# Carrying the gate in every feature: one 512-column pass a tile in the aggregation of a graph layer

## The reference

```python
xn  = layernorm(x)
neigh = xn[dst]
w   = sigmoid(relu(neigh @ W1 + b1) @ W2 + b2)     # one gate a node
num = segment_sum(neigh * w, src)                  # 256 sums a node
den = segment_sum(w, src)                          # one sum a node
out = where(den > 0, num / max(den, 1e-12), 0)
x2  = x + out + mix(xn)
```

## Time and profile before

| | |
|---|---|
| median of 3 runs | 1849.69 us |
| the profiled execution, its own time | 1852.44 us |
| its span, first to last instruction | 1850.3 us |
| TensorE busy (matmul) | 1487.4 us, 80% |
| VectorE busy | 1346.5 us, 73% |
| ScalarE busy | 820.7 us, 44% |
| matmuls of `aggregate` | 4802 |
| mean granted TensorE clock | 0.915 of full speed |

### The profile page before, as it was taken

One profiled execution on the slowest core, in us unless ns is written; L12 is line 12 of the kernel. 1 busy time (PEld: TensorE's weight loads), 2 busy tenths in 40 slices (PEclk: granted clock), 3 DMA queues, 4 the chain that ended last, 5 costly groups with the idle time before them and its releaser, 6 DMA issues.

```text
span 1850.3 us, 40316 instructions
## 1 busy us (share of the span) xinstructions
PE 1487.4 (80%) x12157; PEld 1373.1 (74%) x12157; DVE 1346.5 (73%) x3891; ACT 820.7 (44%) x1979; POOL 750.7 (41%) x727
## 2 busy tenths in 40 slices
PE   0327776755659999999999999999999659999897
PEld 0226665644549988888888989888888649998786
DVE  6966999989937777777777777776777546676555
ACT  1114343424635555454544454544545325554443
POOL 1497677774431222222212122222213143337776
PEclk9958787856779999999999999999999869999999
DMA  7000000002334110110101010110101055543442
GB/s 173 12 0 1 1 1 1 1 3 78 129 100 142 37 43 35 37 43 31 46 31 48 31 43 34 43 37 32 45 31 48 35 168 138 138 117 96 121 124 77
DMA packets 68021, 108.67 MB, mean 59 GB/s; under 512 B 14164, under 2 KB 47707, under 8 KB 67705
## 3 DMA queue, kind: packets, MB, share of 16 engines
q1 hardware_dynamic: 49720, 56.19, 11.1%
q0 software_dynamic: 18240, 51.74, 7.9%
HBM read 52.41 MB, written 57.47 MB: 59 GB/s over the span
## 4 chain that ended last, share of the span: by engine, by line
PE 59%; issue 15%; POOL 9%; DVE 8%; ACT 3%; DMA 3%; SPq 1%; DVEq 1%; another core or an unknown queue 0%; POOLq 0%; ACTq 0%
PE turned L1386 17%; PE front L1386 15%; PE turned L1368 9%; POOL acc_mem L766 5%; DVE sort_mem L1674 4%; PE turned L1522 4%; PE front L1522 4%; PE front L1542 4%; ACT a_ring L1124 2%; POOL tab_mem L752 2%; DMA gath_mem<-in_dst 1%; PE front L1415 1%; PE turned L1515 1%; PE front L1420 1%; DVE sort_mem L1682 1%
## 5 line engine op out<-in xcount | busy, mean ns | idle before, releaser
L1780 DVE TENSOR_TENSOR sort_mem<-lane_bf,sort_mem 128x512 bf16<-128x512 bf16 x1372 | 500.3, 406 | 204.8 <-PE turned L1368 190.2
L1124 ACT ACTIVATE a_ring<-turned 128x512 fp32r<-128x512 f32 (+2 forms) x686 | 368.8, 544 | 442.1 <-PE turned L1368 437.4
L1386 PE MATMUL turned<-y_all,a_ring 128*128 128x258 f32 x2450 | 388.9, 296 | 30.6 <-ACT a_ring L1124 30.6
L1386 PE MATMUL front<-y_all,a_ring 128*128 128x258 f32 x2352 | 378.9, 298 | 13.0 <-ACT a_ring L1124 11.8
L1386 PEld LDWEIGHTS turned<-y_all,a_ring 128*128 128x128 f32 x2450 | 317.6, 190 | 36.4 <-ACT a_ring L1124 33.7
L1674 DVE TENSOR_TENSOR sort_mem<-sort_mem 128x320 f32<-128x320 f32 (+2 forms) x568 | 326.8, 637 | 3.0
L1386 PEld LDWEIGHTS front<-y_all,a_ring 128*128 128x128 f32 x2352 | 305.9, 189 | 27.7 <-ACT a_ring L1124 23.7
L1368 PE MATMUL turned<-sort_mem 128*128 128x128 bf16 (+1 forms) x2695 | 258.9, 217 | 2.7 <-DVE sort_mem L1780 2.5
L851 POOL COPY feat_mem<-node_id 128x1 int32 (+1 forms) x49 | 9.0, 183 | 445.7 <-DVE list_at L1889 445.7
L1368 PEld LDWEIGHTS turned<-sort_mem 128*128 128x128 bf16 x2695 | 147.8, 98 | 36.6 <-DVE sort_mem L1780 3.6
L2070 DVE COPY acc_mem<-feat_mem 128x1796 f32 x112 | 122.7, 1098 | 24.8 <-issue 24.8
(11 more groups left out here) (256 smaller groups left out, 2293.5 us busy)
## 6 DMA issues: line engine op xcount, KB each, us to landing
base<-token_lists SPq DMA_DIRECT2D x54, 258.0 KB
base<-token_lists SPq DMA_DIRECT2D x54, 130.0 KB
gated_rows<-tab_mem SPq DMA_DIRECT2D x49, 128.5 KB, 2.9
late_mem<-mixed_rows SPq DMA_DIRECT2D x49, 128.0 KB
mixed_rows<-base SPq DMA_DIRECT2D x12, 512.0 KB, 3.5
feat_mem<-in_L_ffn_expert_w SPq DMA_DIRECT2D x18, 256.0 KB, 6.1
base<-in_x SPq DMA_DIRECT2D x1, 3136.0 KB
base<-in_x SPq DMA_DIRECT2D x1, 2352.0 KB
```

Of the source, the lines that this page charges most:

```text
L1124: nc.scalar.activation(a_ring[:, k % 2, :, :].rearrange("p s n -> p (s n)")[:, 0:width], ps_a[k % 2][:, 0:width], ACT.Copy).then_inc(S["a_ ...
L1386: last = nc.tensor.matmul(ps_agg[odd], a_ring[:, k % 2, n, :], y_part(t, part), start=(t == 0 and part == 0), stop=(t == BLOCKS - 1 and pa ...
L1780: nc.vector.tensor_tensor(hot[:, k % 2, 0:pairs, 0:lanes, :], lane_bf[:, 0:lanes, :].unsqueeze(1).broadcast_to([P, pairs, lanes, 2]), edge ...
```

## The change

Both parts become 256 columns wide, so that a tile of `y_all` is 512 columns, and one matmul of 512 columns takes the place of two of 258. Its output fills one PSUM bank: the sums of the high parts on the left, of the low parts on the right. The gate's column leaves `y_all`. Instead the gate is added to every feature (`y_bias` becomes `(x_bias + 1) * gate`), so a row is `gate * (xn + 1)`. As the features of xn sum to zero, the sum over all 512 columns is 256 times the sum of the gates: ScalarE takes it while it copies the sums, with `accum_out`. VectorE makes minus a 256th of it and the larger of a 256th and 1e-12 (two small operations at step 4), the reciprocal at step 5, joins high part, low part and the negative at step 6, and makes x2 at step 7. Y_TILE goes from 516 to 512.

```diff
-PART = DIM + 2
-Y_TILE = 2 * PART
+Y_TILE = 2 * DIM
...
-LEAD = dict(den=4, over_den=5, x2=6, stats=8, ...
+LEAD = dict(den=4, over_den=5, join=6, x2=7, stats=8, ...
...
-        sums = dense(ROW)
+        sums = dense(Y_TILE)
...
-        ps_agg = [turned[:, 2 * BANK:2 * BANK + PART], bank(3)[:, 0:PART]]
+        ps_agg = [turned[:, 2 * BANK:2 * BANK + Y_TILE], bank(3)[:, 0:Y_TILE]]
...
-        N_NORM, N_ROUTE = 4, 9
-        X2_LINK = 3
+        N_NORM, N_ROUTE = 6, 9
+        JOIN_LINK, X2_LINK = 4, 5
...
             nc.gpsimd.tensor_tensor(y_scale, x_rstd, gate, ALU.mult).then_inc(S["y_params"], 1)
-            nc.gpsimd.tensor_tensor(y_bias, x_bias, gate, ALU.mult).then_inc(S["y_params"], 1)
+            nc.gpsimd.tensor_scalar(y_bias, x_bias, 1.0, None, ALU.add).then_inc(S["y_params"], 1)
+            pool.wait_ge(S["y_params"], 2)
+            nc.gpsimd.tensor_tensor(y_bias, y_bias, gate, ALU.mult).then_inc(S["y_params"], 1)
...
-                nc.gpsimd.tensor_tensor(y_part(t, 1), y_out[:, t % Y_SLOTS, :], y_part(t, 0).bitcast(F32), ALU.subtract)...
+                nc.gpsimd.tensor_tensor(y_part(t, 1), y_out[:, t % Y_SLOTS, 0:DIM], y_part(t, 0).bitcast(F32), ALU.subtract)...
...
-                nc.scalar.activation(y_part(t, 0), y_out[:, s, :], ACT.Copy).then_inc(S["hi_ready"], 1)
+                nc.scalar.activation(y_part(t, 0), y_out[:, s, 0:DIM], ACT.Copy).then_inc(S["hi_ready"], 1)
...
-                    act.wait_ge(S["norm_step"], N_NORM * (rounds - 2) + X2_LINK)
-                nc.scalar.activation(sums, ps_agg[1 - odd][:, 0:ROW], ACT.Copy).then_inc(S["sums_kept"], 1)
+                    act.wait_ge(S["norm_step"], N_NORM * (rounds - 2) + JOIN_LINK)
+                nc.scalar.activation(sums, ps_agg[1 - odd], ACT.Copy, accum_out=den[:, 0:1]).then_inc(S["sums_kept"], 1)
...
-                    for part in range(2):
-                        last = nc.tensor.matmul(ps_agg[odd], a_ring[:, k % 2, n, :], y_part(t, part), start=(t == 0 and part == 0),
-                                                stop=(t == BLOCKS - 1 and part == 1))
+                    last = nc.tensor.matmul(ps_agg[odd], a_ring[:, k % 2, n, :], y_parts(t), start=(t == 0), stop=(t == BLOCKS - 1))
...
-                        nc.vector.tensor_scalar(den[:, 0:1], sums[:, DIM:ROW], 1e-12, None, ALU.max).then_inc(S["norm_step"], 1)
+                        weight, share = den[:, 0:1], 1.0 / DIM
+                    nc.vector.tensor_scalar(den[:, 1:2], weight, -share, None, ALU.mult).then_inc(S["norm_step"], 1)
+                    nc.vector.tensor_scalar(den[:, 2:3], weight, share, 1e-12, ALU.mult, ALU.max).then_inc(S["norm_step"], 1)
+                if j == LEAD["over_den"]:
+                    dve.wait_ge(S["norm_step"], links + 2)
...
+                    nc.vector.reciprocal(den[:, 3:4], den[:, 2:3]).then_inc(S["norm_step"], 1)
+                if j == LEAD["join"]:
...
+                        nc.vector.scalar_tensor_tensor(x2[slot], sums[:, 0:DIM], den[:, 1:2], sums[:, DIM:Y_TILE], ALU.add,
+                                                       ALU.add).then_inc(S["norm_step"], 1)
                 if j == LEAD["x2"]:
+                    dve.wait_ge(S["norm_step"], links + JOIN_LINK)
...
-                    nc.vector.scalar_tensor_tensor(x2[slot], of, den[:, 1:2], mixed_in[slot], ALU.mult, ALU.add)...
+                    nc.vector.scalar_tensor_tensor(x2[slot], x2[slot], den[:, 3:4], mixed_in[slot], ALU.mult, ALU.add)...
```

More of the change, by code:

```diff
@@ L134 @@
 RUNS = ((0, 4), (4, 8), (8, 12), (12, GROUP))
-LEAD = dict(den=4, over_den=5, x2=6, stats=8, spread=10, norm=17, turn=18, turned=19, router=21, hidden=22, logits=24,
+LEAD = dict(den=4, over_den=5, join=6, x2=7, stats=8, spread=10, norm=17, turn=18, turned=19, router=21, hidden=22, logits=24,
             peak=28, exp=30, probs=37, top=40, top_exp=42, index=43, share=46, marks=48, rank=50, place=54)
@@ L215 @@
 assert HALF // 2 < TAIL < HALF // 2 + 2 * P
-SCRATCH = 25 * Y_TILE + PART
+SCRATCH = 13158
 GATHERED = GROUP * ROW
@@ L273, in y_part, with y_parts @@
         def y_part(t, k):
-            at = home_of_tile(t) * Y_TILE + k * PART
-            return y_all[:, at:at + PART]
+            at = home_of_tile(t) * Y_TILE + k * DIM
+            return y_all[:, at:at + DIM]
+        def y_parts(t):
+            at = home_of_tile(t) * Y_TILE
+            return y_all[:, at:at + Y_TILE]
         mixed_in = [late_mem[:, s * DIM:(s + 1) * DIM] for s in range(2)]
@@ L426, in gps_layer @@
         to_lane, round_up, round_down = (in_front(1) for _ in range(3))
-        den, stats, mean_var, rstd, logit_max, exp_l = (after(n) for n in (2, 6, 2, 2, 1, EXPERTS))
+        den, stats, mean_var, rstd, logit_max, exp_l = (after(n) for n in (4, 6, 2, 2, 1, EXPERTS))
         exp_sum, top, top_i, top_f, top_w = after(2), after(8), after(8).bitcast(U32), after(2), after(3)
@@ L1818, in normalise @@
                         dve.nop().then_inc(S["slot_free"], 1)
-                        nc.vector.tensor_scalar(den[:, 0:1], acc_mem[:, bass.ds(ROW * b + DIM, 1)], 1e-12, None, ALU.max).then_inc(S["norm_step"], 1)
+                        weight, share = acc_mem[:, bass.ds(ROW * b + DIM, 1)], 1.0
                     else:
                         dve.wait_ge(S["sums_kept"], n + 1)
-                        nc.vector.tensor_scalar(den[:, 0:1], sums[:, DIM:ROW], 1e-12, None, ALU.max).then_inc(S["norm_step"], 1)
-                    dve.wait_ge(S["norm_step"], links + 1)
-                    dve.nop().then_inc(S["slot_free"], 1)
-                if j == LEAD["over_den"]:
-                    nc.vector.reciprocal(den[:, 1:2], den[:, 0:1]).then_inc(S["norm_step"], 1)
+                        weight, share = den[:, 0:1], 1.0 / DIM
[3 more added lines that the diff above has]
+                    dve.wait_ge(S["norm_step"], links + 2)
+                    dve.nop().then_inc(S["slot_free"], 1)
+                    nc.vector.reciprocal(den[:, 3:4], den[:, 2:3]).then_inc(S["norm_step"], 1)
+                if j == LEAD["join"]:
+                    if not isinstance(listed, int) or listed > 0:
+                        dve.wait_ge(S["row_listed"], 32 * listed)
+                        dve.nop().then_inc(S["slot_free"], 1)
+                    if cut_path:
+                        nc.vector.tensor_scalar(x2[slot], acc_mem[:, bass.ds(ROW * b, DIM)], den[:, 1:2], None, ALU.add).then_inc(S["norm_step"], 1)
+                    else:
+                        nc.vector.scalar_tensor_tensor(x2[slot], sums[:, 0:DIM], den[:, 1:2], sums[:, DIM:Y_TILE], ALU.add,
+                                                       ALU.add).then_inc(S["norm_step"], 1)
                 if j == LEAD["x2"]:
-                    dve.wait_ge(S["norm_step"], links + 2)
+                    dve.wait_ge(S["norm_step"], links + JOIN_LINK)
                     dve.nop().then_inc(S["slot_free"], 1)
@@ L1831, in normalise @@
                     dve.nop().then_inc(S["slot_free"], 1)
-                    if not isinstance(listed, int) or listed > 0:
-                        dve.wait_ge(S["row_listed"], 32 * listed)
-                        dve.nop().then_inc(S["slot_free"], 1)
-                    of = acc_mem[:, bass.ds(ROW * b, DIM)] if cut_path else sums[:, 0:DIM]
-                    nc.vector.scalar_tensor_tensor(x2[slot], of, den[:, 1:2], mixed_in[slot], ALU.mult, ALU.add).then_inc(S["norm_step"], 1)
+                    nc.vector.scalar_tensor_tensor(x2[slot], x2[slot], den[:, 3:4], mixed_in[slot], ALU.mult, ALU.add).then_inc(S["norm_step"], 1)
                     dve.wait_ge(S["norm_step"], links + X2_LINK)
```

11 lines of the change are left out of this document (5 added, 6 removed).

## The result

The changed kernel takes 1878.35 us, the median of 4 runs (1873.92 to 1882.12), beside 1851.59 for the kernel before (1848.67 to 1855.93): 1.015 times as long, 95% interval 1.0125 to 1.0175. Measured again later beside the kernel before (1882.98 against 1870.12) it is 1.006 (1.0045 to 1.0076). The change makes the kernel slower, by about 1%; the prediction was 1820, a gain. Part of the first difference is probably not the change, as the sums copies show.

What follows compares the result with a forecast made beforehand. TensorE's matmuls were taken to set the round's length. Tile savings less head delays gave -1.21 us a pair, -29.0 over 24 pairs, -29.5 with the small terms: 1820.2 us from the median 1849.7, range 1807 to 1850.

Steps and rivals of the forecast that it cites:

- The tile: TensorE's matmuls at L1386: one of 512 columns at 0.217 us replaces two passes at 0.240, saving 0.023 a tile.
- The middle estimate: TensorE's 512-column matmul at 0.223 us if the cost above streaming is paid once; a tile then saves 0.017.
- The ScalarE chain: Head of a round: longer sums copy with accumulator delays group 1's tile copy by 0.40 us, group 2 by 0.14 without table load.
- table round: Every second round, beginning with a table load on ScalarE; forecast to change by 0.25 - 0.71 = -0.46 us.
- The late release: Round without table load: group 2's ring copy releases TensorE 0.85 us after the build's modelled end, passing on 0.14 of 0.40.
- The VectorE chain: Head of a round: join moves x2's end and later marks by 0.63 us; group 7's build +0.25 with table load, otherwise hidden.
- sign of being wrong: Forecast is wrong if pitch exceeds 0.225, the late release moves with matmuls behind it, or marks hold up several groups a round.
- The smaller terms: Outside the rounds: join behind the last round's DMA wait +0.63 us; extra GpSimd operation of about 0.5 hidden by the sort.
- (C): Rival: matmul priced by the column, 0.238 a tile, nothing pays for the longer sums copy; slower, 1859 us; chance 0.12.
- (B): Rival: gain given back at the head, ScalarE's 0.40 passes through every round, tile 0.223; 1837 us; chance 0.23.
- (D): Rival: head costs nothing, ScalarE's copy and VectorE's join fit into today's waits; 1795 us; chance 0.04.
- (E): Rival: a 512-column matmul costs 0.131 us, saving 0.109 a tile, VectorE becomes the bound; 1706 us; chance 0.01.

Runs made afterwards that it cites:

- e2: Changed kernel with each 512-column matmul split into two of 256: 1877.2 us, 1.0136 of the kernel before.
- e5: e3 with the old sums copy of 257 columns and no accumulator, so only the merged matmul: 1865.27 us, 0.9983 of the kernel before.
- e3: Changed kernel with the wide join replaced by a one-column operation, x2 made from the high sums alone: 1866.56 us, 1.0049 of the kernel before.

## Why the prediction was wrong

**The tile, where the sum failed first.** The step reads "I take 0.217, the lower end: that row is the nearest in what it does". The row is of another type (f32 activations and weights of the experts): there a column costs 0.217/256 = 0.85 ns, in the fp32r matmul 0.120/258 = 0.47. That its 256 columns and 512 fp32r columns came out close was chance, and what the two have in common, one instruction over a long stream, was not what sets the price. Nearest was the 258-column fp32r matmul of the same line: e2 shows 118 ns for 256 columns and 231 for 512, twice as much less 5. A tile is 0.234; the excess of the 258-column pass over its streaming, which I took to be paid once an instruction, is nearly all paid by the column. The saving is 0.006 in place of 0.023: with my 66 tiles a pair that alone turns -1.21 into -0.09, and with the 16 tiles ahead of group 7's build, where TensorE alone would then stand at 0.30, to about 0. (The middle estimate, 0.223, does not follow from the rows either: by the 0.217 of the earlier trace rows the excess of 258 columns is 0.011, which gives 0.228. And from group 2's matmuls to group 5's build there are six tiles, not four: 0.05 a pair.)

The Trainium skill (TensorE: Matmul & The Clock Gate, Back-to-back issue gap) gives N/2.4 + 2.5 ns as the isolated gap. The traces agree in bf16 (0.215 for 512 columns against its 0.216, and 0.109 to 0.113 for 258 against 0.110), and not in fp32r (0.231 and 0.120). That the merge saves almost nothing, which follows from it, held; the formula is short by 15 ns on a merged tile and by 20 on one of two passes.

**The ScalarE chain** was sized about rightly: "Together the copy of group 1's tile behind it comes 0.40 us later"; in the table round TensorE's wait grew by 0.32, the build of group 3 came 0.28 later (median), and the copy with its accumulator cost 0.43 a pair between e5 and e3. (The prediction had 0.40 + 0.14.) The late release on which the 0.14 rested is not there after the change, where the ring copy at 956.22 runs two tiles without a gap. What the prediction put at nothing is what a longer wait may do to the clock: one fall costs 1.1 to 1.4 us, so three, as in the first profile, are 3 to 4 us of the 16.

**The VectorE chain, where the sign was lost.** The step said "x2's end moves by 0.63" and then that the ring copy of 978.02 hides the marks' delay in the round without table load. One more row of the timeline before, x2 in the round of the earlier trace rows:

```profile
976.10 0.49 DVE L1836 SCALAR_TENSOR_TENSOR feat_mem<-sort_mem,feat_mem,late_mem 128x256 f32<-128x256 f32 x1 [0.37 <-DMA token_lists<-feat_mem,list_at]
```

Measured from the sums copy of such a round, x2 ended 4.19 us later before (976.10 + 0.49 - 972.40) and 5.41 after (960.55 + 0.49 - 955.63): 1.22 more. 0.82 of it is the join and its result, 0.48 + 0.34, where I had taken 0.14 for the latter from operations of one column; 0.40 is that the DMA, too, landed later from that point. I had put the DMA's wait ahead of the join and seen in it a cover for the small operation; it is no cover for what stands behind it. The build of group 6 then waits 1.11 us, and the ring copy hides none of it. Of the 0.40, 0.26 is GpSimd's: the second of the two instructions that issue this DMA, before and after, takes 0.22 longer and ends 2.00 us behind the start of the sums copy in place of 1.74:

```profile
973.18 0.96 POOL L855 DMA_INDIRECT token_lists<-feat_mem,list_at  x1 [0.30 <-issue]
```

```profile
956.45 1.18 POOL L859 DMA_INDIRECT token_lists<-feat_mem,list_at  x1 [0.30 <-issue]
```

In the medians of the rounds without table load it is 0.96 and 1.18, too.

For the table round the step said: TensorE alone at +0.03 at the build of group 7, "VectorE holds it to +0.25". It came 0.50 later. The two delays did not hide behind one another, they added: 0.28 by ScalarE at the build of group 3, of which 0.26 is left at that of group 5, and then another 0.25 up to that of group 7, where VectorE's marks come last. That is the prediction's own sign of being wrong, marks that hold up more than one group a round. In the other round the build of group 7 came 0.30 later where the sum, with the right price of a tile, has about 0.1. So the two rounds lose 0.2 each beyond that sum, which by itself comes to about 0 a pair; 0.4 and the rounds at the lower clock make up most of the +0.5 to +0.7 (an estimate, from medians of the first profile of each kernel).

**The smaller terms.** Behind the last round the kernel after waits as that of the earlier trace rows did, 4.79 us against 4.85:

```profile
1503.11 0.48 DVE L1838 SCALAR_TENSOR_TENSOR feat_mem<-sort_mem,feat_mem 128x256 f32<-128x256 f32 x1 [4.79 <-DMA token_lists<-feat_mem,list_at]
```

The join comes behind that wait, as forecast; the stages behind vary by more between profiles than the 0.63 counted there. The GpSimd operation can't be seen in a front that itself varies by 17 us.

**The rivals.** (C), slower because a matmul is priced by the column, at 1859, had the sign and the mechanism on TensorE, with a chance of 0.12. Its place for the loss was wrong: it put +0.31 a pair on the table round, by ScalarE, and nothing on VectorE. Against the median of before it forecast 9 us, and beside the kernel before in the second comparison it is 11; that the size fits is partly luck, as its terms at the head do not. Its threshold of 0.234 is where the tile came out. (B)'s delay by ScalarE came in both kinds of round (0.28 and 0.29 at the build of group 3), but without a table load it was made up by the late releases that went; (D) and (E) fall with the pitch. The range up to 1850 left C out because I had let a row of another type outweigh the same line's own price.

**What stays open.** Why GpSimd's instruction takes 0.22 longer in the round without table load (VectorE's marks run beside more of it after the change), what made the late releases of before and took them away, whether the longer wait is what lowers the clock, and what makes the sort 17 us longer in one profile than in another; none was tried by itself. In the first comparison the medians differ by 27 us and the rounds of the profiles by 16: the rest is not explained by the rounds.

## What to carry to other kernels

Price a wider matmul from the same line's own type and pitch: if it doubles its columns and the price is proportional, the merge gives nothing, and everything hung on it is pure cost. Before adding an operation to an in-order engine, look for what is behind it in the queue and what it waits for: here moving the join three steps, past the marks, was worth about twice what the change had cost. Measure such a move in the kernel before, too: 0.5 of its 1.2 us a pair was to be had without the change. Two delays on two engines in one round can add, even where each looks hidden behind the other. And when an earlier stage varies by more than the change is worth, compare the changed stage itself between two events of the same trace.

## What the runs showed that I had not expected

- An fp32r matmul cost 118 ns for 256 columns, 120 for 258 and 231 for 512, in bf16 0.109 to 0.113 us for 258 and 0.215 for 512. The first matmul of a group, 84 ns dearer in fp32r, is no dearer in bf16; the weight loads in the profiles took 189 to 191 ns in fp32r and 97 in bf16.
- The wait of an operation on 256 columns for the one ahead of it on VectorE was 0.34 us (13.4 us in 40), not the 0.14 between one-column operations.
- The same sort, with the same operations at nearly the same median time (674 and 678 ns), began its last one at 507.9 or 525.1 us in two profiles of one program.
- In six fp32r profiles TensorE, else at full clock, waits 1.60 or 1.61 us at the head of 23 rounds, and in one to four of these the granted clock then fell to 0.50; with waits of 1.29 to 1.31, in four profiles, it never did.
